# Splitting an edge sort: the smaller keys of every two runs go on, the rest are only counted

## What is computed

```python
M = 8192                                  # nodes
src = concat([edge_index[0], arange(M)])  # 262144 edges, drawn from 0 .. 16383
dst = concat([edge_index[1], arange(M)])
e = leaky_relu(a_src[src] + a_dst[dst])
alpha = exp(e - segment_max(e, dst)[dst]) / segment_sum(exp(...), dst)
agg = segment_sum(h[src] * alpha, dst)    # 4 heads, softmax over each node's edges
scores = layernorm(agg + b_gat).mean(heads)
w = softmax(top 2 of 4 scores)
out = sum over 4 experts of gate(w) * (gelu(x @ W1 + b1) @ W2 + b2)
```

## Time and profile before

| what | us |
|---|---|
| median of three executions | 1712.96 |
| the profiled execution | 1709.23 |
| its span | 1707.4 |
| DVE busy | 1354.5 (79%) |
| PE busy | 907.1 (53%) |
| POOL busy | 897.8 (53%) |
| ACT busy | 487.5 (29%) |
| attention and early sort | 24 to 333 |
| first to last `hidden` of the 143 tiles | 397.0 to 685.7 |
| convolution | 695 to 838 |
| dense experts, first to last bias | 863.5 to 992.6 |
| edge rounds, first scores to last sums | 1001.3 to 1611.6 |
| routing, to the end | 1612.3 to 1707.4 |

### The profile page before, as it was taken

One profiled execution on the slowest core, in us unless ns is written; L12 is line 12 of the kernel. 1 busy time (PEld: TensorE's weight loads), 2 busy tenths in 40 slices (PEclk: granted clock), 3 DMA queues, 4 the chain that ended last, 5 costly groups with the idle time before them and its releaser, 6 DMA issues. The chain is left out here.

```text
span 1707.4 us, 37553 instructions
## 1 busy us (share of the span) xinstructions
PE 907.1 (53%) x13315; PEld 706.6 (41%) x13315; DVE 1354.5 (79%) x2698; ACT 487.5 (29%) x974; POOL 897.8 (53%) x889
## 2 busy tenths in 40 slices
PE   0322232226888888255589966555556555555400
PEld 0222222214666666255422245555455554555400
DVE  6899999989899988499721168888788887888799
ACT  0222132214555544366444422111111211111100
POOL 0055555543666655100057777777777777777100
PEclk9555555556666665577699965555555555555555
DMA  7000000011111111421020111111111111111001
GB/s 161 0 23 22 22 22 20 24 43 29 42 42 44 42 39 38 76 64 51 16 23 10 14 11 13 12 12 12 17 12 12 12 12 17 12 12 12 5 6 43
DMA packets 113549, 46.92 MB, mean 27 GB/s; under 512 B 92407, under 2 KB 108495, under 8 KB 112738
## 3 DMA queue, kind: packets, MB, share of 16 engines
q0 software_dynamic: 27648, 20.64, 6.8%
q1 hardware_dynamic: 83666, 21.85, 6.7%
q10 hardware_dynamic: 2064, 2.10, 0.6%
HBM read 29.11 MB, written 15.90 MB: 26 GB/s over the span
## 5 line engine op out<-in xcount | busy, mean ns | idle before, releaser
L285 POOL DMA_INDIRECT edges_rows<-table,edges_src x576 | 548.1, 952 | 196.3 <-issue 195.6
L185 DVE TENSOR_TENSOR sorting_keys<-sorting_keys 128x1024 f32<-128x1024 f32 (+1 forms) x392 | 372.5, 992 | 17.5 <-ACT sorting_keys L266 15.7
L674 POOL DMA_INDIRECT y_rows<-mixture_yt,mixture_xin x143 | 179.5, 1255 | 131.3 <-ACT mixture_yt L889 84.5
L669 POOL DMA_INDIRECT x_rows<-mixture_sent,mixture_slot x128 | 158.3, 1236 | 156.0 <-DVE mixture_slot L731 117.5
L1992 ACT ACTIVATE edges_hotT<-edges_h 128x1024 bf16<-128x1024 bf16 x74 | 71.7, 1021 | 411.1 <-PE edges_h L1896 411.1
L993 PE MATMUL mixture_bank<-mixture_xT,sorting_w_part 128*128 128x128 bf16 x858 | 117.6, 257 | 49.7 <-DVE mixture_hidden L816 28.7
L993 PEld LDWEIGHTS mixture_bank<-mixture_xT,sorting_w_part 128*128 x858 | 85.0, 105 | 85.6 <-issue 76.8
L1749 DVE TENSOR_TENSOR all_eo<-edges_back,edges_ub 128x1024 f32 x16 | 19.6, 1224 | 113.8 <-PE edges_back L1863 113.8
L1958 PE MATMUL edges_acc<-edges_term_parts,edges_work 128*128 128x20 bf16 x1728 | 51.6, 179 | 92.2 <-DVE edges_term_parts L1611 92.2
L1958 PEld LDWEIGHTS edges_acc<-edges_term_parts,edges_work 128*128 128x128 bf16 x1728 | 49.1, 104 | 96.9 <-issue 96.9
L1896 PE MATMUL edges_h<-edges_ident,edges_work 128*128 128x128 bf16 x592 | 69.0, 310 | 31.0 <-DVE edges_work L1710 31.0
(11 more groups left out here) (394 smaller groups left out, 2309.5 us busy)
## 6 DMA issues: line engine op xcount, KB each, us to landing
edges_rows<-table,edges_src POOLq DMA_INDIRECT x576, 2.4
mixture_xin<-x_rows SPq DMA_DIRECT2D x143, 49.0 KB, 1.8
all_eo<-y_rows SPq DMA_DIRECT2D x16, 256.0 KB, 4.0
y_rows<-mixture_yt,mixture_xin POOLq DMA_INDIRECT x143, 2.5
sorting_w<-in_L_ffn_w_dram SPq DMA_DIRECT2D x4, 512.0 KB, 8.5
x_rows<-mixture_sent,mixture_slot POOLq DMA_INDIRECT x128, 2.3
out_dram<-all_x_sb SPq DMA_DIRECT2D x8, 256.0 KB, 2.6
constants_src_i<-in_L_ffn_edge_index_dram SPq DMA_DIRECT2D x1, 1024.0 KB, 5.2
```

What stands on the lines that cost most here:

```text
L185: self.st.mark(dve.tensor_tensor(target[half], source[0], source[1], (ALU.min, ALU.max)[half]))
L285: pool.indirect_dma_start(to, None, rows, where).then_inc(done, 16)
L669: pool.indirect_dma_start(x_rows, bass.IndirectOffsetOnAxis(ap=slot[g % 2][:, c, t:t + 1], axis=0), now[c][:, t, :], None).then_inc(scatte ...
L674: pool.indirect_dma_start(y_rows, bass.IndirectOffsetOnAxis(ap=xin[j % XB][:, ROWX - 2:ROWX - 1].bitcast(U32), axis=0), yt[j % YB][:, :], ...
```

## The change

1. **Keys.** Real edges get the smallest keys, then dropped ones, then last-source edges (field `dst + 2N`).
2. **Sort.** Levels 1 to 6 are as before. Where two sorted runs of 64 are to be merged, `part_runs` writes the smaller 64 of the 128 to one half array (1024 columns) and the larger 64 to a `rest`. Only the smaller half is sorted on: 40 more early exchanges at half width, seven merge stages at half width (196 units in place of 210, key transposes 112 in place of 224; `due` lets the first tile wait for 20 units, not 14). The rest gets 13 half-width exchanges of its own in the stages (`sort_rest`), so that each run of 128 is sorted, and goes to HBM and back.
3. **Counting.** Last-source edges are no longer counted in the edge rounds. Of each rest run of 128 the 96 largest are counted during the dense experts: three batches of 2048 keys a group, per batch two DVE comparisons (`hot_lasts`) and 16 matmuls (`count_lasts`). `number_lasts` makes their numbers ahead of that. `add_bias` of a group comes after the next group's batches.
4. **Overflow loops**, with trip counts from the keys, at least one each, between the dense experts and the edge loop: last-source keys that were in the smaller halves (`late`), those among the 32 smallest of a rest run (`few`), and real edges that were in the larger halves (`strays`, one column of 128 edges a trip, 31 DVE steps with PE and ACT in between). `times` is read ahead of the strays.
5. **Edge loop.** As before, without `one_hot_last` and `count_last`; a key row has 64 partitions.

```diff
+    def part_runs(self, dve):
+        d, to = 1 << self.RUN, 1 - self.now(None)
+        v = self.keys[1 - to][:, :].rearrange("p (b r h d) -> p b r h d", r=2, h=2, d=d)
+        near, far = (w.rearrange("p (b r d) -> p b r d", r=2, d=d) for w in (self.keys[to][:, 0:SC], self.rest()))
...
+            for out, choice in ((near, (ALU.min, ALU.max)[r]), (far, (ALU.max, ALU.min)[r])):
+                self.st.mark(dve.scalar_tensor_tensor(out[:, :, r, :], flip, -1.0, keep, ALU.mult, choice))
...
+        self.width = SC
...
-    def due(self, tiles, units, first=14):
+    def due(self, tiles, units, first=20):
...
                     want_turn(s, 2 + n)
+                    sort.sort_rest(dve)
...
+            def hot_lasts(nth, n16, b16, at, spare, alone=False):
+                wait_apart(dve, last_counted, nth + (BATCHES if alone else 1), spare)
+                equal_to(hot_last[at], node_ps, P, n16).then_inc(last_made, 1)
+                equal_to(hot_block[at], node_ps, T, b16).then_inc(last_ready, 1)
...
-            with dve.Fori(0, FFN_GROUPS) as g:
-                add_bias(g)
...
+            count_rest(0)
+            with dve.Fori(1, FFN_GROUPS) as g:
+                count_rest(g)
+                add_bias(g - 1)
+            add_bias(FFN_GROUPS - 1)
...
+            with dve.Fori(0, late_trips) as r:
...
+            with dve.Fori(0, few_trips) as r:
...
+            dve.wait_ge(closed, 1)
+            dve.tensor_copy(times[:, :], times_ps).then_inc(times_read, 1)
...
+            with dve.Fori(0, strays) as c:
...
             one_hot(0)
-            one_hot_last(st, 0)
...
                         st.mark(dve.tensor_copy(old, now[:, :]))
-                        one_hot_last(st, nxt)
                         dve.wait_ge(now_ready, at(u, g))
...
                     if e >= LAG or not first:
                         out_product(n - LAG, (e - LAG) % K)
+                    if e < BATCHES:
+                        count_lasts(g * BATCHES + e, e)
                     if e == K - 1 and not first:
                         turn_back(g - 1)
...
+            def count_lasts(nth, at):
+                wait_apart(pe, last_ready, nth + 1, spare)
+                for t in range(GB):
+                    ins = pe.matmul(times_ps, hot_last[at][:, t, :], hot_block[at][:, t, :], start=False, stop=False)
+                ins.then_inc(last_counted, 1)
...
                     spread_flags(nxt)
-                    count_last(nth + 1, nxt)
```

More of the change, by code:

```diff
@@ new lines, in rest, with sort_rest @@
+    def rest(self):
+        return self.keys[self.far][:, SC:EC]
+    def sort_rest(self, dve):
+        if self.far_steps > 2 * self.RUN:
+            return
+        self.wait_written(dve)
+        source, self.far = self.rest(), 3 - self.far
+        if self.far_steps == self.RUN:
+            self.merge_runs(dve, source, self.rest(), self.RUN)
+        else:
+            left = (self.RUN - 1 if self.far_steps < self.RUN else 2 * self.RUN) - self.far_steps
+            v, w = (x.rearrange("p (b h d) -> p b h d", h=2, d=1 << left) for x in (source, self.rest()))
+            for half in range(2):
+                self.st.mark(dve.tensor_tensor(w[:, :, half, :], v[:, :, 0, :], v[:, :, 1, :], (ALU.min, ALU.max)[half]))
+        self.far_steps += 1
@@ L828, in _ @@
                     sort.wait_turned(dve, n, s, n)
-                    for m in range(k - 11):
+                    for m in range(k - sort.LEVEL):
                         sort.across(dve, k, m, n)
@@ L838, in _ @@
                 for n in range(2):
-                    for m in range(sort.WHOLE, 11):
+                    for m in range(sort.WHOLE, sort.LEVEL):
                         sort.below(dve, m, n)
@@ new lines, in count_rest @@
+            def count_rest(g):
+                for j in range(BATCHES):
+                    n16, b16 = (eo_pairs[:, bass.ds(g * stride + n * span + j * GB, GB), :] for n in range(2))
+                    hot_lasts(g * BATCHES + j, n16, b16, j, spare)
+            runs = rest[:, 0:SC].rearrange("p (b r d) -> p r b d", r=2, d=2 << Sort.RUN)
+            few, many = starts.FEW, (2 << Sort.RUN) - starts.FEW
+            rounds = FFN_GROUPS // 2
+            for r, (far, near) in enumerate(((slice(few, None), slice(0, few)), (slice(0, many), slice(many, None)))):
+                part = slice(r * rounds, (r + 1) * rounds)
+                numbers = last_i[:, r * rounds * span:(r + 1) * rounds * span]
+                st.mark(dve.tensor_copy(few_keys[:, r, :, :], runs[:, r, :, near]))
+                number_lasts(st, numbers.rearrange("p (b d) -> p b d", d=many), last_n16[:, part, :, :], last_b16[:, part, :, :],
+                             runs[:, r, :, far], numbers.rearrange("p (g w) -> p g w", w=span))
```

463 lines of the change are left out of this document (352 added, 111 removed).

## The result

The change takes **1766.85 us** (1766.13 to 1767.15, four executions) beside 1713.2 for the kernel before in the same series (1712.33 to 1715.47): a ratio of 1.0308, 95% interval 1.0292 to 1.0324. It is slower, as forecast; 1760 was said, between 1690 and 1806. The profiled execution has a span of 1764.9 us, 57.5 more than before.

The account below looks back on a forecast made before the run. Bounds: DVE in attention, DVE with PE close behind in the experts, PE in the dense experts, POOL in the edge loop. -92 + 2 + 141 = +51, less 1, on 1709.23 gave 1759; with the median's offset 1760, range 1690 to 1806.

Parts of the forecast that it names:

- POOL sets the edge loop: Edge loop: POOL's unbroken gathers, 1.26 us each and 20.2 per round, set its end, so lighter DVE rounds buy nothing after lap one.
- The stop: Edge loop: POOL stands still for 140 us after its first 12 rounds, waiting for the second lap's sources from DVE.
- rounds of 20 us: Sign that the forecast is right: edge rounds of 20 us in the last two laps, in which DVE waits for rows.
- The graph's loss: Edge loop: its end comes at 1753 in place of 1611.6, without the gain before the convolution: +141 us.
- 120 + 36 = 156: Ahead of the edge loop: +120 us for dense experts with counts and numbering, 36 for the overflow loops.
- The 1159: Edge loop: first scores forecast at 1001 + 120 + 36 + 2 = 1159 us, on the old clock without the 92 gained.
- Attention and first tile: Attention and early sort: half-width exchanges bring the first `hidden` from 397 to 347 us, 40 and 10 less.
- The expert stretch: Experts: PE becomes the pace at 1.59 us a tile and clock 0.66, taking 250 us in place of 292.
- rival 4: Expert stretch gains nothing because PE stays at 1.80 us a tile: 35 us more, 1795; chance 0.09.
- Rival 1: Experts run free at 1.4 us a tile, 50 us more won; with dense experts at 14.8, 1690; chance 0.20.
- Rival 2: Edge loop: DVE, not POOL, bounds it, gathers going faster when DVE does less; rounds at 14.9, 1712; chance 0.05.
- Rival 3: Dense experts: PE's clock stays at 0.50, period 18.2, 35 us more, 1795, or 1809 with loops at upper bound; chance 0.16.

## Why the prediction was right, and where its terms were off

1. **POOL sets the edge loop.** Right, and shown from both sides: without the counts in the rounds nothing is won, and what comes off ahead of the first round comes off the end (19.3 and 97.9 us less stop, 21.3 and 94.0 less time). The stop was 126.2 us where 140 stood. One sign came only in part: rounds of 20 us, in which DVE waits for rows, had been said for the last two laps and show in the last ten rounds alone, since POOL's lead carries the rounds before.
2. **The graph's loss, +141 said, +124 measured.** The chain from first scores to the end came out: sources 87 us behind (89 said; a round was 2.2 us shorter, where 1.7 stood), from POOL's restart to the last sums 505 (505 said). What was off lies ahead of the first scores. Counted from POOL's first gather they came 141.0 us later than before (279.2 for 138.2), where 120 + 36 = 156 had been said. Up to the last bias it was 109.1 for 120: the period was 15.0 and not 16, with a clock of 0.88 and not a middle value, and `number_lasts` took 4.5 (793.6 to 798.05) in place of 7.6. The 1 us for register loads in that 7.6 had no row, and no run shows them as a time of their own. From the last bias to the first scores it was 31.9 (40.6 for 8.7) where 36 stood; the strays were 20.8 (22 said). The 1159 also holds a +2 without a name. The only +2 of the prediction is the convolution's, and the sum adds that one again: counted once, the graph's +141 is +139 and the sum +49.
3. **Attention and first tile.** -50 said, -53.1 measured; the scatter -43.0 for -40. The exchanges that cover less did not cost anything visible.
4. **The expert stretch, 250 said, 275 measured** (first `hidden` to last output, 343.9 to 618.7, as in the 292 before). This is the term that failed. I kept the mean clock of 0.66 and so a pitch of 1.59 us; the clock in the stretch was 0.61. PE's timeline shows tile after tile at the slow pitch of the earlier trace rows with hardly a gap:

```profile
487.88 0.84 PE L1049 MATMUL mixture_bank<-mixture_xT,sorting_w_part 128*128 128x128 bf16 x6
...
489.67 0.84 PE L1049 MATMUL mixture_bank<-mixture_xT,sorting_w_part 128*128 128x128 bf16 x6
...
491.48 0.83 PE L1049 MATMUL mixture_bank<-mixture_xT,sorting_w_part 128*128 128x128 bf16 x6
```

So it went 25 of the 35 us towards rival 4, and from first to last `hidden` it is 271 / 143 = 1.90 a tile, with the key transposes in it (20.7 us, 24 said). The clock alone doesn't make up the 25: the prediction's own working with 0.61 gives some 1.65 a tile, 9 us more (an estimate). PE also stood still for 30 of the 270 us, 13.8 of them in 28 waits for `hidden`, and the sum had no term for that. Nor is it shown that the clock fell because DVE does less: in the run with one more instruction per exchange DVE was busy for 208 of the same 270 us in place of 166.5, and the clock was 0.58.
5. **The sum.** -70 + 4 + 124 is +58 in place of -92 + 2 + 141 = +51. The 1760 is so near to 1766.85 because two errors, 22 and 17 us (15 with the +2 counted once), had opposite signs. That is luck: the terms were good to some 20 us, not to 7.
6. **The rivals.** Rival 1 (experts run free) didn't occur: PE became the limit, at a lower clock (0.61 for 0.66). Rival 2, the rounds set the loop, is wrong for the change, and its reason, faster gathers, is wrong everywhere (1.25 us each); but in the two runs with all sources ahead of the first round the rounds do set it, at 14.7 to 14.8 each, where 14.9 stood. Rival 3 (cold dense experts) is refuted by a period of 15.0 at 0.88. The prediction took the rule of the Trainium skill's page on TensorE (TensorE: Matmul & The Clock Gate, "What's actually happening"), that the throttled clock is the default and activity releases it, to mean 1.2 GHz for this loop. The trace has the loop mostly at 2.4, and the expert stretch, where PE is busy for 240 of 270 us, mostly at 1.2. In direction the loop agrees with the page: the level falls after PE's longest wait (the rows stand in the last section). Why the expert stretch stays low, with hardly a wait, was not tried and is open.

## What to carry to other kernels

When an engine runs ahead of a loop and its queue is full from end to end, the loop's busy engine can lose nearly a quarter of its work for nothing (120 of DVE's 498 us in the edge rounds), while every microsecond put ahead of the loop's first round is paid once the lead is used up. So look first for who gives the engine that runs ahead its next permission, and move that permission forward: here two changes of order, with no work less, turned a loss of 54 us into a gain of 40, until the rounds themselves became the limit. And where two engines take turns in a loop, one batch of the next turn made ahead of the wait keeps both at work.

## What had not been expected of the hardware

PE's granted clock fell, from 0.66 to 0.61, in a stretch where its busy share rose from 85% to 89%. Part of that share is the clock itself, since the same matmuls take longer at the low level; but from 356 to 376 us PE was busy for 18.6 of 20 us, and the granted clock was 0.50 all along. In the dense experts it was 0.88 at 74%, and there the trace shows where it falls: each full turn has one wait of 3.29 us for DVE's comparison, and in ten of the 14 turns the first output product after that wait takes 1.42 to 1.97 us. The same product takes 1.07 at the high level, which is back by the next one:

```profile
828.72 1.97 PE L2128 MATMUL edges_acc<-edges_work,edges_u 128*64 128x512 f32 x2
...
832.76 1.07 PE L2128 MATMUL edges_acc<-edges_work,edges_u 128*64 128x512 f32 x2
```

With DVE's order turned, the waits for the comparisons were at most 1.07 us and the granted clock was 1.00. Taking DVE's load away from beside POOL did not speed up the gathers: 1.25 us from one to the next with DVE full, half idle or idle, in every kernel here.
